# Two graph layers on one core: the masks of a group in one operation, fewer waits, fewer signals

## The reference

```python
h = jnp.maximum(_layernorm(x, axis=-1), 0.0)
# layer 1: attention over the edges of a node, 4 heads of 32 channels
x = nodes @ W + b_lin
feat = jnp.concatenate([x[snd], x[rcv]], axis=1).reshape(-1, H, 2 * C)
logits = jax.nn.leaky_relu(jnp.sum(feat * alpha, axis=-1), negative_slope=0.2)
e = jnp.exp(logits - seg_max[rcv])
att = e / denom[rcv]                      # denom: sum of e over a node's edges
out = jax.ops.segment_sum(att[:, :, None] * sent.reshape(-1, H, C), rcv, num_segments=n) + bias
# layer 2: a message network on every edge
ef = jax.nn.relu(edge_attr @ We1 + be1) @ We2 + be2
ef = ef * jax.nn.sigmoid(ts @ Wt + bt)
combined = jnp.concatenate([x[row], ef], axis=1)
msg = jax.nn.relu(combined @ Wn1 + bn1) @ Wn2 + bn2
out = jax.ops.segment_sum(msg, col, num_segments=x.shape[0])
```

## Time and profile before

| | us |
|---|---|
| median of 3 runs | 2840.2 |
| the profiled execution | 2840.72 |
| its span | 2838.9 |

### The profile page before, as it was taken

The page is one execution under the profiler, slowest core; times in us unless marked ns, Lnnn a source line. Parts: engine busy times, 40 slices in busy tenths (PEclk is TensorE's granted clock), DMA queues, the critical chain, the costliest instruction groups (busy, mean ns, idle before and its releaser), DMA issues.

```text
span 2838.9 us, 30406 instructions
## 1 busy us (share of the span) xinstructions
PE 1705.1 (60%) x8785; PEld 1185.5 (42%) x8785; DVE 1536.6 (54%) x5409; ACT 588.7 (21%) x1218; POOL 1601.2 (56%) x1703
## 2 busy tenths in 40 slices
PE   1444545444444444444644877787787787777778
PEld 1333334233333333333434544554454554454556
DVE  1455556554555545556754555555555555555557
ACT  1530000000000000000235333333333233333333
POOL 6425666665566665656063566666666665566650
PEclk6765555555555555555667888887888778888889
DMA  4201221221122111211042333333333333344332
GB/s 122 71 21 40 46 45 44 46 45 43 39 46 46 43 44 42 46 42 45 1 114 71 105 106 95 106 109 110 109 110 111 111 96 100 107 110 112 109 105 79
DMA packets 102330, 212.33 MB, mean 75 GB/s; under 512 B 30944, under 2 KB 65238, under 8 KB 92183
## 3 DMA queue, kind: packets, MB, share of 16 engines
q0 software_dynamic: 53120, 109.70, 15.7%
q1 hardware_dynamic: 46411, 99.73, 12.3%
q10 hardware_dynamic: 2636, 0.98, 0.2%
HBM read 197.40 MB, written 12.88 MB: 74 GB/s over the span
## 4 chain that ended last, share of the span: by engine, by line
PE 31%; DVE 23%; another core or an unknown queue 21%; issue 19%; ACT 4%; DVEq 1%; POOL 0%; DMA 0%; ACTq 0%; SPq 0%; POOLq 0%
DVE acc L670 9%; PE pair L1424 6%; PE bank L1433 6%; PE bank L1444 5%; PE pair L1418 4%; PE pair L973 4%; DVE onehot L665 2%; DVE acc L1627 2%; DVE onehot L1586 2%; DVE pre L1612 1%; PE pair L960 1%; DVE ef L1593 1%; PE bank L937 1%; ACT hidden L1503 1%
## 5 line engine op out<-in xcount | busy, mean ns | idle before, releaser
L1367 POOL DMA_INDIRECT acc<-table,index x830 | 786.1, 947 | 533.6 <-DVE pre L1612 268.5
L472 POOL DMA_INDIRECT rows<-table,index x782 | 742.7, 950 | 539.8 <-issue 214.5
L1627 DVE TENSOR_TENSOR acc<-acc,bank 128x128 f32 x832 | 239.5, 288 | 411.6 <-remote 188.0
L665 DVE TENSOR_SCALAR onehot<-iota_row,dst_rel 128x128 f32<-128x128 f32 x808 | 235.6, 292 | 408.3 <-remote 326.3
L1424 PE MATMUL pair<-hidden,we 128*128 128x512 f32 x416 | 281.6, 764 | 210.6 <-ACT hidden L1503 152.3
L973 PE MATMUL pair<-onehot,rows 128*128 128x128 f32 x1616 | 382.3, 411 | 0.0
L973 PEld LDWEIGHTS pair<-onehot,rows 128*128 128x128 f32 x1616 | 328.0, 301 | 68.6 <-issue 61.1
L1433 PEld LDWEIGHTS bank<-wn1b,ef 128*128 128x128 f32 x1664 | 273.3, 237 | 193.4 <-issue 100.6
L670 DVE TENSOR_TENSOR acc<-acc,pair 128x256 f32 x832 | 349.5, 420 | 5.4 <-PE pair L973 1.8
L1433 PE MATMUL bank<-wn1b,ef 128*128 128x128 f32 x1664 | 280.6, 324 | 52.4 <-DVE ef L1593 44.1
L1444 PE MATMUL bank<-onehot,msg 128*128 128x128 f32 x1664 | 261.9, 309 | 13.4 <-ACT msg L1516 8.8
(11 more groups left out here) (170 smaller groups left out, 1466.6 us busy)
## 6 DMA issues: line engine op xcount, KB each, us to landing
ts<-in_ts SPq DMA_DIRECT2D x52, 1024.0 KB
ea<-in_ea_t SPq DMA_DIRECT2D x52, 512.0 KB
acc<-table,index POOLq DMA_INDIRECT x830
rows<-table,index POOLq DMA_INDIRECT x782
table<-feat SPq DMA_DIRECT2D x16, 195.0 KB
table<-proj SPq DMA_DIRECT2D x12, 256.0 KB, 2.3
table<-x_rows SPq DMA_DIRECT2D x11, 256.0 KB, 2.3
out<-x_rows SPq DMA_DIRECT2D x11, 256.0 KB
```

Source lines behind the costliest of these rows:

```text
L472: gp.indirect_dma_start(rows0[:, n % (RING * TG), :], None, table1, bass.IndirectOffsetOnAxis(index[:, n:n + 1], 0)).then_inc(half_in[g % ...
L665: dve.tensor_scalar(mask_of(n), iota_row[:, :], dst_rel[:, n:n + 1], None, ALU.is_equal).then_inc(early_ready if n // TG in EARLY else oh0, 1)
L1367: gp.indirect_dma_start(rows[:, g % RG1, t, :], None, table, bass.IndirectOffsetOnAxis(index[:, n:n + 1], 0)).then_inc(gathered[g % RG1], 16)
L1627: dve.tensor_tensor(acc[:, ds(v, P)], acc[:, ds(v, P)], bank[6 + g % 2][:, t * P:(t + 1) * P], ALU.add).then_inc(acc1, 1)
```

## The change

There are four edits. (1) In both layers the four masks of a group are made by one `tensor_tensor` comparison of 128x512 instead of four `tensor_scalar` comparisons of 128x128. In layer 1 this one stands ahead of the four additions instead of one mask ahead of each addition; the semaphore `oh0` counts groups. The 24 masks of the last six groups stay as they are. (2) In layer 2 the waits are left out that an earlier wait on the same engine, or a chain of others, implies. The semaphore `oh1` is gone. (3) A unit's statistics, means and normalised blocks signal once, at their last instruction, and `bn_aggr` of a unit waits once for all its `bn_stats`. (4) ACT's scaling in the last two rounds of layer 1 signals once a group.

```diff
                     for j in range(size(w)):
-                        dve.bn_stats(moments0[:, w * UA + j, :], taken(w)[:, j, :]).then_inc(moments_in, 1)
+                        last = dve.bn_stats(moments0[:, w * UA + j, :], taken(w)[:, j, :])
+                    last.then_inc(moments_in, 1)
+                    dve.wait_ge(moments_in, w + 1)
                     for j in range(size(w)):
-                        dve.wait_ge(moments_in, ahead(w) + j + 1)
-                        dve.bn_aggr(mean_var0[:, w * UA + j, :], moments0[:, w * UA + j, :]).then_inc(mean_done, 1)
+                        last = dve.bn_aggr(mean_var0[:, w * UA + j, :], moments0[:, w * UA + j, :])
+                    last.then_inc(mean_done, 1)
...
+                def masks_of(g):
+                    dve.tensor_tensor(onehot[:, g % 2], iota_row[:, :].unsqueeze(1).broadcast_to([P, TG, P]),
+                                      dst_rel[:, g * TG:(g + 1) * TG].unsqueeze(2).broadcast_to([P, TG, P]), ALU.is_equal).then_inc(oh0, 1)
...
                     dve.wait_ge(agg0, g + 1)
+                    if g + 2 < EARLY.start:
+                        masks_of(g + 2)
                     for t in range(TG):
-                        if g + 2 < EARLY.start:
-                            mask((g + 2) * TG + t)
                         add(g * TG + t, at[t])
...
-                        pe.wait_ge(oh0, (g + 1) * TG)
+                        pe.wait_ge(oh0, g + 1)
...
                 def first_product(g):
...
-                    if g >= 2:
-                        pe.wait_ge(r1, g - 1)
...
                     pe.wait_ge(r1, g + 1)
-                    if g >= 2:
-                        pe.wait_ge(efd, g - 1)
...
                         pe.wait_ge(rows1, WORK1)
-                    if g >= 2:
-                        pe.wait_ge(radd, g - 1)
...
                     pe.wait_ge(r2, g + 1)
-                    pe.wait_ge(oh1, (g + 1) * TG)
-                    if g >= 2:
-                        pe.wait_ge(acc1, (g - 1) * TG)
...
                     act.wait_ge(h1, g + 1)
-                    if g >= 2:
-                        act.wait_ge(h2, g - 1)
...
-                    if g >= 2:
-                        act.wait_ge(efd, g - 1)
+                    if g == 2:
+                        act.wait_ge(efd, 1)
...
                     act.wait_ge(radd, g + 1)
-                    if g >= 2:
-                        act.wait_ge(agg1, g - 1)
...
                 def masks(g):
-                    if g >= 2:
-                        dve.wait_ge(agg1, g - 1)
-                    for t in range(TG):
-                        q = g * TG + t
-                        dve.tensor_scalar(onehot[:, g % 2, t, :], iota_row[:, :], dst_rel[:, q:q + 1], None, ALU.is_equal).then_inc(oh1, 1)
+                    dve.tensor_tensor(onehot[:, g % 2], iota_row[:, :].unsqueeze(1).broadcast_to([P, TG, P]),
+                                      dst_rel[:, g * TG:(g + 1) * TG].unsqueeze(2).broadcast_to([P, TG, P]), ALU.is_equal)
...
                     dve.wait_ge(gt, g + 1)
-                    if g >= 2:
-                        dve.wait_ge(z1, g - 1)
...
-                    if g >= 2:
-                        dve.wait_ge(r2, g - 1)
```

More of the change, by code:

```diff
@@ L662, in rescale, with early_mask @@
                     settle()
-                def mask(n):
-                    dve.tensor_scalar(mask_of(n), iota_row[:, :], dst_rel[:, n:n + 1], None, ALU.is_equal).then_inc(early_ready if n // TG in EARLY else oh0, 1)
+                def early_mask(n):
+                    dve.tensor_scalar(mask_of(n), iota_row[:, :], dst_rel[:, n:n + 1], None, ALU.is_equal).then_inc(early_ready, 1)
+                def masks_of(g):
+                    dve.tensor_tensor(onehot[:, g % 2], iota_row[:, :].unsqueeze(1).broadcast_to([P, TG, P]),
+                                      dst_rel[:, g * TG:(g + 1) * TG].unsqueeze(2).broadcast_to([P, TG, P]), ALU.is_equal).then_inc(oh0, 1)
                 def add(n, v):
@@ L712, in maxima @@
                     dve.memset(acc2[SH * HC:, 0, NPAD:], 0.0).then_inc(zero_done, 1)
-                for n in range(2 * TG):
-                    mask(n)
+                masks_of(0)
+                masks_of(1)
                 maxima(0)
@@ L785, in first_vector @@
                             for n in range((EARLY.start * RG + k * len(EARLY)) * TG // RG, (EARLY.start * RG + (k + 1) * len(EARLY)) * TG // RG):
-                                mask(n)
+                                early_mask(n)
                     scan_rows(r)
@@ L871, in turn @@
                 def turn(w):
-                    pe.wait_ge(normed_in, ahead(w + 1))
+                    pe.wait_ge(normed_in, w + 1)
                     if w >= 2:
@@ L970, in sum_group @@
                     else:
-                        pe.wait_ge(scaled0, (g + 1 - SPANS[CLOSE][0]) * TG * SH)
+                        pe.wait_ge(scaled0, g + 1 - SPANS[CLOSE][0])
                     for t in range(TG):
@@ L1057, in root @@
                         act.wait_ge(sel_done, 3)
-                    act.wait_ge(mean_done, ahead(w + 1))
+                    act.wait_ge(mean_done, w + 1)
                     act.activation(std0[:, kept(w)], mean_var0[:, kept(w), 1:2].rearrange("p b o -> p (b o)"), ACT.Sqrt,
@@ L1067, in normalize @@
                         at = w * UA + j
-                        act.activation(normed[:, w % 2, j, :], taken(w)[:, j, :], ACT.Relu, scale=rstd0[:, at:at + 1],
-                                       bias=shift0[:, at:at + 1]).then_inc(normed_in, 1)
+                        last = act.activation(normed[:, w % 2, j, :], taken(w)[:, j, :], ACT.Relu, scale=rstd0[:, at:at + 1],
+                                              bias=shift0[:, at:at + 1])
+                    last.then_inc(normed_in, 1)
                 def keep(w):
@@ L1155, in scale_group @@
                             row = row_of(g * TG + t)[:, h * HC:(h + 1) * HC]
-                            act.activation(row, row, ACT.Copy, scale=edge_w[:, r % 2, (g - SPANS[r][0]) * TG + t, h:h + 1]).then_inc(scaled0, 1)
+                            last = act.activation(row, row, ACT.Copy, scale=edge_w[:, r % 2, (g - SPANS[r][0]) * TG + t, h:h + 1])
+                    last.then_inc(scaled0, 1)
                 def fetch(r, half):
@@ L1389, in turn @@
                 def turn(u):
-                    pe.wait_ge(hrelu1, before(u + 1))
+                    pe.wait_ge(hrelu1, u + 1)
                     if u >= 2:
@@ L1464, in root @@
                 def root(u):
-                    act.wait_ge(mean1, before(u + 1))
+                    act.wait_ge(mean1, u + 1)
                     act.activation(std1[:, held(u)], mean_var[:, held(u), 1:2].rearrange("p b o -> p (b o)"), ACT.Sqrt,
@@ L1474, in normalize @@
                         at = u * UB + j
-                        act.activation(normed_of(u)[:, j, :], taken1(u)[:, j, :], ACT.Relu, scale=rstd1[:, at:at + 1],
-                                       bias=shift1[:, at:at + 1]).then_inc(hrelu1, 1)
+                        last = act.activation(normed_of(u)[:, j, :], taken1(u)[:, j, :], ACT.Relu, scale=rstd1[:, at:at + 1],
+                                              bias=shift1[:, at:at + 1])
+                    last.then_inc(hrelu1, 1)
                 def keep(u):
@@ L1546, in statistics @@
                     for j in range(members(u)):
-                        dve.bn_stats(moments[:, u * UB + j, :], taken1(u)[:, j, :]).then_inc(moments_done, 1)
+                        last = dve.bn_stats(moments[:, u * UB + j, :], taken1(u)[:, j, :])
+                    last.then_inc(moments_done, 1)
+                    dve.wait_ge(moments_done, u + 1)
                     for j in range(members(u)):
-                        dve.wait_ge(moments_done, before(u) + j + 1)
-                        dve.bn_aggr(mean_var[:, u * UB + j, :], moments[:, u * UB + j, :]).then_inc(mean1, 1)
+                        last = dve.bn_aggr(mean_var[:, u * UB + j, :], moments[:, u * UB + j, :])
+                    last.then_inc(mean1, 1)
                 def scale(u):
```

## The result

The kernel after took 2754.94 us (median of 4 runs, 2751.23 to 2759.49), the kernel before 2842.71 in the same job (4 runs, 2838.53 to 2846.76): ratio 0.9692, 95% interval 0.967 to 0.9714. The forecast of 2874 us and its range from 2785 up were wrong. The profiled execution of after took 2751.23 us, its span is 2749.1.

What follows compares the result with a forecast made beforehand. The prediction took PE's late signals and POOL's stops to bound the kernel. Its terms, 20 + 20 + 8 - 12 - 5 + 3 = +34 us on 2840.72, gave 2874 us; own range 2850 to 2905, whole 2785 to 2925.

Steps and rivals of the forecast that it cites:

- What bounds the kernel: Both layers: no engine is near its span; PE's late signals and POOL's stops set the time, not summed compute.
- Masks, layer 1, +20: Layer 1: one comparison ahead lengthens DVE's group by 0.41 us, paid twice a round over 25 rounds: +20 us.
- The sign that was set: Layer 1: among the signs that the forecast was right, this stretch would be 30 to 50 us longer.
- DVE's busy time: DVE, both layers: 1640 masks go and 410 longer ones come, 283 us of work for 476.
- Contact with POOL, +20 and +8: Gathers meeting the two-input mask are held up: layer 1 0.2 us at four restarts a round, +20; layer 2 +8 us.
- Masks, layer 2, -12: Layer 2: one mask of 0.69 us replaces 0.87 us, 0.18 less, counted in one group in three: -12 us.
- Waits left out, -5: Layer 2: implied waits never held an engine, only their instructions go, at most 0.1 us a group: -5 us.
- One signal a unit, +3: Units: `bn_aggr` waits for all `bn_stats`, about 0.12 us later in 54 units; bounds 0 and +6, taken +3 us.
- Faster by fewer late signals: Rival, chance 0.08: dropping about 1600 mask signals and extra waits shortens remote waits by 171 us, to 2670 us.
- Faster, by layer 2: Rival, chance 0.20: PE and DVE carry layer 2's cycle, -37 - 21 and layer 1 free: 2783 us, or 2812 with half.
- Both signs named as proof against the forecast: Remote waits shrinking by more than 50 us in sum; runs of more than 12 gathers between layer 2 stops.
- The summed +34 us: Whole kernel: all terms together, 20 + 20 + 8 - 12 - 5 + 3, added to 2840.72 us.

Runs made afterwards that it cites:

- e15: Kernel after with layer 1's mask as two two-input operations of 128x256 ahead of the additions; late signals; ratio to before 1.0105, layer 1 1313 us.
- e7: Kernel after with layer 1's mask made by four tensor_scalar operations ahead of the additions, on the chip without late signals; ratio to before 1.0089.
- e6: Kernel before, unchanged, run on the chip without late signals; 2170.16 us.
- e5: Kernel after, unchanged, run on the chip without late signals; ratio to before 1.0202.
- e8: Kernel after with layer 2's masks as four tensor_scalar operations of 128x128, on the chip without late signals; ratio to before 1.0119.
- e11: Kernel after with layer 1's mask as four two-input tensor_tensor operations of 128x128 ahead of the additions; late signals; ratio to before 0.996.
- e3: Kernel before with only layer 2's implied waits left out, DVE's masks still signalling; late signals; ratio to before 0.9956.
- e4: Kernel before with only edits (3) and (4), fewer signals in the units and in ACT's scaling; late signals; ratio to before 1.0014.
- e2: Kernel before with its four masks a group kept, only the fourth signalling, in both layers; late signals; ratio to before 1.0002.
- e12: Kernel after with four tensor_scalar masks in both layers; late signals; ratio to before 1.0089, layer 2 1252 us.
- e16: Kernel before with one 128x256 memset on POOL ahead of each group's gathers in layer 1; late signals; ratio to before 0.9978.
- e17: Kernel before with two 128x256 memsets on POOL ahead of each group's gathers in layer 1; late signals; ratio to before 0.9984.
- e14: Kernel after with a 128x128 copy on DVE ahead of layer 1's mask in each group; late signals; ratio to before 0.9843.

## Why the prediction was wrong

- *What bounds the kernel.* Right as a reading: late signals and POOL's stops. The step that failed is the next one, in the sum: it took the late signals as a fixed background, onto which each edit adds its local price. On such a chip the kernels differ in which signal of a round is late, and that is worth more than all local terms: the seventh group's was late in every round before and in none after, DVE's waits of over 3 us ahead of a group of layer 1 fell from 349 to 124 us, and the stretch by 65 us where the sum had +40. It goes the other way as easily: with the mask in two halves (e15) the last group's is late in every round, which takes 52.6 us in place of 46.2. Why the one mask moves it in this way stays open.
- *Masks, layer 1, +20.* The lead was right in size (0.61 us, the group 2.68 in place of 2.28) and wrong in effect. Without late signals a longer chain costs nothing (e7, 2.86 us a group: layer 1 in 991.30 us, with 2.27 in e6 991.60); with them it is drowned in the pattern. The sign that was set, 30 to 50 us more in layer 1, did not come.
- *DVE's busy time.* The prediction had the masks fall from 476 to 283 us of work, and by their durations they do. The busy time fell by 37 us alone, since the old masks of layer 1 lay in DVE's waits between additions or on top of them: in layer 1 DVE is busy for 702 us before and 700 after.
- *Contact with POOL, +20 and +8.* That the mask holds gathers up was right, and it is the whole effect where no signal is late, +26 and +19 to +22 us. Layer 2 was under-sized. The gather of 766.01 began 0.23 us into the mask and lasted 0.33 longer, that of 768.84 began 0.13 into one of 768.71 and lasted 0.44 longer, each about 0.12 less than the rest of the mask. So do 243 of the 245 gathers of after that start in a mask with over 0.15 us to go; in sum they last 34 us longer in layer 1 and 33 in layer 2, for the forecast's 20 and 8. Gathers that start inside an addition of layer 1, whose second input is a sum that PE has just written (`pair`, not in SBUF), are not longer (200 of them, 0.8 us in sum).
- *Masks, layer 2, -12.* No such gain: e5 has 18.6 us more than e8. The masks took 0.685 us as priced. At 128 columns the two forms cost the same: 292 ns with a scalar (L665 before), 290 with two tensors (e11).
- *Waits left out, -5.* Alone -13 us (-21 to -4) where signals are late (e3); nothing to be seen where they are not (e8's layer 2 has 999.7 us, before 996.1). With the mask's signal gone as well, layer 2 had 38 us less on the mean of the late profiles, 26 to 30 within one job: this joint effect had no term.
- *One signal a unit, +3.* Right: +4 us (-3 to +12) in e4, and 0.6 us of 100.8 in e5. Three statistics now end at 46.70 and `bn_aggr` starts 0.03 later; before it started 0.09 ahead of the end:

```profile
46.03 0.67 DVE L551 BATCH_NORM_STATS2 moments<-x_rows 128x6 f32<-128x128 f32 x3
46.73 0.31 DVE L555 BATCH_NORM_AGGREGATE mean_var<-moments 128x2 f32<-128x6 f32 x3
```

- *The rivals.* "Faster by fewer late signals" had the outcome, to half its size, with the wrong reason: signals that are not sent save nothing (e2). "Faster, by layer 2" had 29 to 58 us and layer 1 free; layer 2 gave 27, but not by the mask's form (e12), and layer 1 gave more. Both signs named as proof against the forecast came: remote waits shrank by more than 50 us, and POOL made runs of more than 12 gathers in layer 2. The summed +34 us is near what the chip without late signals gave, +45, but that is another chip than the one forecast for.

## What to carry to other kernels

Where waits are ended by "remote" and come back in a pattern, an edit's local price says little (layer 1 had +40 us in the sum and came out at -65): find which signal of a cycle is late, how near the next ones are to being so, and give the forecast a range in both directions by a whole stop. Price a two-input DVE operation beside a running gather engine by how much it lengthens the gathers that start inside it, times their number; on the chip without late signals that accounted for 23.6 of the 25.7 us in layer 1 and for all 22.2 in layer 2 (23.0). And measure a small change on more than one chip: 0.97 and 1.02 are the same kernel. A pattern read from one profiled execution is to be set beside other executions with the same code before an edit is given the credit.

## What the runs showed of the hardware

- The same program took 2174 us on one chip and 2837 to 2853 us in the other jobs, with nearly the same busy time on DVE, ACT and POOL (1525.2 and 1536.6, 585.3 and 588.7, 1612.2 and 1601.2 us). Most of the difference is idle time: before has 326 us of "remote" waits ahead of DVE's masks and 294 us ahead of ACT's `relu_hidden`, e6 none of either, and the units ahead of layer 1 take 197.5 and 100.8 us. PE's busy time differs too (1705.1 and 1566.1 us, at a mean granted clock of 0.70 and 0.78). What makes a chip or a job such, no run here shows.
- The lateness is in the trace's own records of the semaphore `agg0`, and not in modelled ends alone: in before, the update for the row products that end at 702.51 stands at 715.60; in e6, between 600 and 650 us, such updates stand 0.01 to 0.02 us behind the products.
- In those jobs PE's signals are mostly prompt in the first microseconds of a run of gathers (18 of the 22 waits of DVE in layer 2 of before whose product ended in the first 4 us ended within 0.6 us of it) and late further on (none of 20 at 10 to 12 us did); one of DVE's arrived in 0.15 us beside running gathers. Of the 56 waits of over 3 us in layer 1 of before, 55 end 0.9 to 2.9 us after POOL's last gather, and POOL starts again within 0.4 us; so the late signals come once POOL has stopped, and POOL stops because they are late.
- A gather that starts inside a comparison of 128x512 with two SBUF inputs lasts longer by the rest of it less 0.12 us (243 of 245 in after).
- A small pause of POOL shifts that pattern (e16, e17). 0.14 us more on DVE ahead of the additions went with 53 us more in layer 1 (e14).
